# A perceiver block on one core: the first two rounds of its pipeline re-ordered

## The reference

```
# 1  cross attention to a context of 128 rows, 16 heads of 32, low rank
x = x + softmax(((LN(x) @ Wq_d) @ W_qk per head) @ (ctx @ Wkv_d).T / sqrt(32)) @ ((ctx @ Wkv_d) @ Wv_u per head)
# 2  self attention, one head of 128
q, k, v = split(LN(x) @ Wqkv + bqkv)
x = x + softmax(q @ k.T / sqrt(128)) @ v @ Wo + bo
# 3  Hadamard transform, 4-bit activations, ternary weights
xh = LN(x) @ hadamard;  s = max|xh| / 7;   xq = clip(round(xh / s), -8, 7) * s
ws = mean|w| per row;   wq = ws * (+1 where w/ws > 0.5, -1 where w/ws < -0.5, else 0)
x = x + xq @ wq.T
```

## Time and profile before

| | |
|---|---|
| median of 3 runs | 330.17 us |
| the profiled execution | 330.35 us, span 328.6 us |
| TensorE busy | 313.8 us, 95% |
| weight loads | 224.2 us, 68% |
| VectorE busy | 239.7 us, 73% |
| ScalarE busy | 212.5 us, 65% |
| GpSimd busy | 88.5 us, 27% |
| granted TensorE clock | 0.998 |

### The profile page before, as it was taken

How to read it: one execution, slowest core, us unless ns; L and a number is a source line. 1 busy time by engine, 2 the same in 40 slices (tenths; PEclk the granted TensorE clock), 3 DMA queues, 4 the chain that set the end, 5 groups by cost and what they waited for, 6 DMA issues and landing times.

```text
span 328.6 us, 8501 instructions
## 1 busy us (share of the span) xinstructions
PE 313.8 (95%) x3157; PEld 224.2 (68%) x3172; DVE 239.7 (73%) x517; ACT 212.5 (65%) x581; POOL 88.5 (27%) x129
## 2 busy tenths in 40 slices
PE   8989799999999999999999999999999999899995
PEld 6765767767576867667675868677675768575754
DVE  1499548686977868786878778686868788786435
ACT  1485858586686768585776867685867858672210
POOL 2000634241232314242213323242422233232320
PEclk9999999999999999999999999999999999999999
DMA  7994003040402203030403012030302020000000
GB/s 229 281 384 140 27 2 128 3 160 0 162 5 75 86 34 128 31 129 0 160 0 129 31 62 98 32 128 29 131 2 68 0 67 2 32 3 32 0 34 32
DMA packets 13481, 25.25 MB, mean 77 GB/s; under 512 B 3216, under 2 KB 3984, under 8 KB 13456
## 3 DMA queue, kind: packets, MB, share of 16 engines
q1 hardware_dynamic: 13456, 24.91, 22.3%
HBM read 20.71 MB, written 4.19 MB: 76 GB/s over the span
## 4 chain that ended last, share of the span: by engine, by line
PE 63%; DVE 21%; issue 5%; ACT 4%; DMA 3%; SPq 2%; POOL 1%; DVEq 1%; POOLq 0%
PE ps L662 13%; PE ps L702 7%; PE ps L609 5%; PE ps L786 5%; DVE mx L426 4%; PE ps L771 4%; PE ps L679 3%; PE ps L706 3%; PE ps L796 3%; PE ps L751 3%; DMA w_rows<-weight 3%; DVE sum_a L435 3%; PE ps L617 2%; PE ps L634 2%; PE ps L641 2%
## 5 line engine op out<-in xcount | busy, mean ns | idle before, releaser
L305 ACT ACTIVATE prob<-ps,nmx,qk_scale 128x128 f32<-128x128 f32 x256 | 96.2, 466 | 52.7 <-DVE nmx L430 52.7
L662 PE MATMUL ps<-had_s,x3t 128*128 128x512 f32 x128 | 58.4, 599 | 0.9 <-ACT x3t L299 0.9
L426 DVE TENSOR_REDUCE mx<-ps 128x8 f32<-128x1024 f32 x32 | 39.0, 1218 | 13.4 <-PE ps L786 13.4
L662 PEld LDWEIGHTS ps<-had_s,x3t 128*128 128x128 f32 x128 | 23.0, 189 | 24.8 <-issue 23.0
L435 DVE TENSOR_REDUCE sum_a<-prob 128x8 f32<-128x1024 f32 x32 | 37.5, 1209 | 2.3 <-ACT prob L305 2.3
L299 ACT ACTIVATE prob_t<-ps 128x512 f32<-128x512 f32 x64 | 35.2, 622 | 5.4 <-PE ps L609 5.4
L609 PE MATMUL ps<-ident,prob 128*128 128x128 f32 x256 | 33.4, 273 | 0.9 <-ACT prob L305 0.8
L702 PE MATMUL ps<-x2t,wqkv_s 128*128 128x128 f32 x256 | 32.7, 281 | 0.8 <-ACT x2t L299 0.8
L292 POOL TENSOR_TENSOR res<-prod,x 128x512 f32<-128x512 f32 x15 | 19.0, 1268 | 50.5 <-DVE prod L539 50.5
L702 PEld LDWEIGHTS ps<-x2t,wqkv_s 128*128 128x128 f32 x256 | 29.8, 191 | 2.5 <-ACT x2t L299 1.5
L288 POOL TENSOR_TENSOR qk_scale<-aux,power 128x1 f32<-128x1 f32 x16 | 8.8, 551 | 81.4 <-DVE aux L505 81.4
(11 more groups left out here) (115 smaller groups left out, 564.7 us busy)
## 6 DMA issues: line engine op xcount, KB each, us to landing
ct<-ctx_cols SPq DMA_DIRECT2D x16, 512.0 KB, 3.7
xt<-x_cols SPq DMA_DIRECT2D x16, 256.0 KB, 2.6
xr<-x_rows SPq DMA_DIRECT2D x16, 256.0 KB, 3.8
y<-res SPq DMA_DIRECT2D x15, 256.0 KB, 2.0
w_rows<-weight SPq DMA_DIRECT2D x1, 1024.0 KB, 8.8
had_s<-hadamard SPq DMA_DIRECT2D x1, 1024.0 KB, 8.6
wqkv_s<-wqkv SPq DMA_DIRECT2D x1, 768.0 KB, 10.2
wqk<-w_qk SPq DMA_DIRECT2D x2, 128.0 KB, 4.0
```

The lines of the kernel that those rows point to most:

```text
L305: last = nc.scalar.activation(prob[:, h, :], ps[:, h // 4, (h % 4) * P:(h % 4) * P + P], ACT.Exp, bias=nmx[:, h:h + 1], scale=qk_scale[:])
L426: V.tensor_reduce(mx[:, h], ps[:, 2 * half:2 * half + 2, :].rearrange("p r (c k) -> p (r c) k", c=EC), AX.X, ALU.max).then_inc(done["mx"], 1)
L662: mm = pe.matmul(ps[:, B4, :], x3t[:, c, :], had_s[:, c, :], start=(c == 0), stop=(c == EC - 1))
```

## The change

Round 0: on TensorE the projection of pair 1 moves ahead of the transposes of pair 0, between 4 and 8 units of filler (10 before), and the scores of pair 1 ahead of u. ScalarE evicts `lat` first, and no longer q_t, ckv and the first quarter of prob_t, which DVE takes. DVE does the weight's sums and scales there, in pieces between its other work, and both halves of pair 1's maxima. The compares of `ternary()` move into round 1, behind the variance of x2; `second_max()` stands right behind them. The ternary transposes and their evictions move from the end of round 0 to the end of round 1, behind the scores of pair 2, and use bank B2 in place of B3. Some waits change with the banks.

```diff
@@ ScalarE
+                if isinstance(i, int) and i == 0:
+                    latents()
                 if cross:
                     after(act, done["nmx"], i * 2)
                     exps(0, 4)
...
-                    pt_copy(0)
+                    if not (isinstance(i, int) and i == 0):
+                        pt_copy(0)
                     pt_copy(1)
...
-                if isinstance(i, int) and i == 0:
-                    for half, bank in ((0, B4), (1, B3)):
+                if self_:
+                    after(act, made["o2t"], i - 1)
+                    after(act, made["wo"], i - 2)
+                    copy(o2t[:], ps[:, B3, 0:P]).then_inc(read["o2t"], 1)
+
+                if isinstance(i, int) and i == 1:
+                    for half, bank in ((0, B4), (1, B2)):
                         act.wait_ge(ternt_made, half + 1)
@@ DVE (weight_sizes, weight_scales: the parts of ternary() by those names, the second with const_row;
@@      row_variance, row_scale, second_max: lines 497 to 510 as functions)
-                if cross:
+                if cross and not (first and i == 1):
                     largest(i, 1)
-                if isinstance(i, int) and i == 0:
+                if first and i == 0:
                     dve.wait_ge(ld_w["b"], 64)
                     V.tensor_copy(bv_wide[:], b_qkv[:, 2:3].to_broadcast([P, P])).then_inc(bvw_done, 1)
+                    dve.wait_ge(made["qt"], 2)
+                    V.tensor_copy(q_t[:], ps[:, B2, :].rearrange("p (c b q) -> p b c q", c=EC, b=2)).then_inc(read["qt"], 1)
+                    dve.wait_ge(made["ckv"], 2)
+                    V.tensor_copy(ckv[:, 1], ps[:, B1, 0:2 * SKV]).then_inc(read["ckv"], 1)
+                    sums(0)
+                    dve.wait_ge(made["pt"], 1)
+                    V.tensor_copy(prob_t[:, 0, :, :], ps[:, 0, :].rearrange("p (c t) -> p c t", c=EC)).then_inc(read["pt"], 1)
+                    row_variance()
+                    weight_sizes()
+                    dve.wait_ge(done["exp"], 2)
+                    row_scale()
+                    sums(1)
+                    dve.wait_ge(made["s"], 2)
+                    largest(1, 0)
+                    largest(1, 1)
+                    weight_scales()
+                if first and i == 1:
                     ternary()
-                    dve.wait_ge(cb_made, 1)
-                    V.tensor_tensor(const_row[:], ps[:, B4, :], bo_row[:], ALU.add).then_inc(const_ready, 1)
+                    second_max()
@@ TensorE
             def hadamard_mean():
                 pe.wait_ge(ld_w["had"], 16)
-                pe.wait_ge(ternt_read, 1)
+                pe.wait_ge(const_ready, 1)
...
             def ternary_transposed(half, bank):
                 pe.wait_ge(tern_done, EC)
                 if half == 0:
-                    pe.wait_ge(const_ready, 1)
+                    pe.wait_ge(row_read, 1)
                 else:
-                    pe.wait_ge(read["ckvk"], 1)
+                    pe.wait_ge(read["u"], 2)
...
                 if front:
+                    if first and i == 2:
+                        pe.wait_ge(ternt_read, 2)
                     pe.wait_ge(ld_xt[1 - par], (k + par + 1) * 16)
...
                 if cross:
                     if first and i == 0:
-                        keep_busy(10, B1)
+                        keep_busy(4, B4)
+                        after(pe, read["lat"], i + 1)
+                        projected()
+                        keep_busy(8, B4)
                     transposed(0)
                     transposed(1)
                 if first and i == 0:
-                    after(pe, read["lat"], i + 1)
-                    projected()
                     wide_bias()
...
+                if first and i == 0:
+                    scores()
+                if cross:
+                    weighted_sum()
...
-                if first and i == 0:
+                if front and not (first and i == 0):
+                    scores()
+                if first and i == 1:
                     ternary_transposed(0, B4)
-                    ternary_transposed(1, B3)
+                    ternary_transposed(1, B2)
```

More of the change, by code:

```diff
@@ L311, in pt_copy, with latents @@
                     copy(prob_t[:, r, :, :], ps[:, r, :].rearrange("p (c t) -> p c t", c=EC)).then_inc(read["pt"], 1)
+                def latents():
+                    after(act, made["lat"], i + 1)
+                    copy(lat[:], ps[:, B2, 0:P + 2 * SKV]).then_inc(read["lat"], 1)
+                if isinstance(i, int) and i == 0:
+                    latents()
                 if cross:
@@ L321, in body @@
                     exps(4, 8).then_inc(done["exp"], 1)
-                if front:
-                    after(act, made["lat"], i + 1)
-                    copy(lat[:], ps[:, B2, 0:P + 2 * SKV]).then_inc(read["lat"], 1)
+                if front and not (isinstance(i, int) and i == 0):
+                    latents()
                 if cross:
@@ L377, in body @@
                     copy(u_t[:], ps[:, B2, :].rearrange("p (c t) -> p c t", c=EC)).then_inc(read["u"], 1)
-                if isinstance(i, int) and i == 0:
-                    for half, bank in ((0, B4), (1, B3)):
-                        act.wait_ge(ternt_made, half + 1)
-                        copy(tern_t[:, 2 * half:2 * half + 2, :],
-                             ps[:, bank, :].bitcast(BF16).rearrange("p (c o) -> p c o", c=2)).then_inc(ternt_read, 1)
                 if self_:
@@ L386, in body @@
                     copy(o2t[:], ps[:, B3, 0:P]).then_inc(read["o2t"], 1)
+                if isinstance(i, int) and i == 1:
+                    for half, bank in ((0, B4), (1, B2)):
+                        act.wait_ge(ternt_made, half + 1)
+                        copy(tern_t[:, 2 * half:2 * half + 2, :],
+                             ps[:, bank, :].bitcast(BF16).rearrange("p (c o) -> p c o", c=2)).then_inc(ternt_read, 1)
             looped(act, body)
@@ L401, in _, with weight_sizes, weight_scales @@
             V.tensor_copy(fold4[:], fold[:].unsqueeze(1).to_broadcast([P, 4, LAT])).then_inc(fold_made, 1)
-            def ternary():
+            def weight_sizes():
                 dve.wait_ge(ld_w["w"], 16)
                 V.tensor_reduce(w_abs[:], w_rows[:], AX.X, ALU.add, apply_absolute_value=True).then_inc(wabs_done, 1)
+            def weight_scales():
                 dve.wait_ge(wabs_done, 1)
@@ L411, in ternary @@
                 V.tensor_copy(w_wide[:], w_scale[:].unsqueeze(2).to_broadcast([P, EC, P])).then_inc(wide_done, 1)
+                dve.wait_ge(cb_made, 1)
+                V.tensor_tensor(const_row[:], ps[:, B4, :], bo_row[:], ALU.add).then_inc(const_ready, 1)
+            def ternary():
                 dve.wait_ge(whalf_done, 1)
@@ L421, in body @@
             def body(i, k, par, front, cross, self_, quant):
+                first = isinstance(i, int)
                 def largest(pair, half):
@@ L435, in sums, with row_variance, row_scale, second_max @@
                     V.tensor_reduce(sum_a[:, h], prob[:, h, :], AX.X, ALU.add).then_inc(done["sum"], 1)
+                def row_variance():
+                    dve.wait_ge(ld_xr[1 - par], (k + par + 1) * 16)
+                    after(dve, made["lat"], i + 1)
+                    V.bn_stats(stat1[:], xr[:, 1 - par]).then_inc(done["stat1"], 1)
+                    dve.wait_ge(ld_w["wq"], 16)
+                    after(dve, done["stat1"], i + 1)
+                    V.bn_aggr(mv1[:], stat1[:]).then_inc(done["mv1"], 1)
+                def row_scale():
+                    after(dve, done["mv1"], i + 1)
+                    after(dve, done["qk_scale"], i)
+                    V.tensor_scalar(aux1[:], mv1[:, 1:2], EPS, float(LAT), ALU.add, ALU.mult).then_inc(done["aux1"], 1)
+                def second_max():
+                    after(dve, made["s2"], i - 1)
+                    V.tensor_reduce(mx2[:], ps[:, B3, 0:SQ], AX.X, ALU.max).then_inc(done["mx2"], 1)
+                    after(dve, done["mx2"], i - 1)
+                    V.tensor_scalar(nmx2[:], mx2[:], -float(D2) ** -0.5, None, ALU.mult).then_inc(done["nmx2"], 1)
                 if self_:
@@ L487, in body @@
                     V.tensor_scalar(qi[:], z[:], ROUND, QMAX, ALU.subtract, ALU.min).then_inc(done["qi"], 1)
-                if cross:
+                if cross and not (first and i == 0):
                     after(dve, done["rsum"], i - 1)
@@ L495, in body @@
                         .then_inc(read["qit"], 1)
[L496 to L510, removed]
+                if front and not (first and i == 0):
+                    row_variance()
+                    row_scale()
+                if self_ and not (first and i == 1):
+                    second_max()
                 if cross:
@@ L631, in body @@
                     if first and i == 2:
-                        pe.wait_ge(row_read, 1)
+                        pe.wait_ge(ternt_read, 1)
                     for c in range(EC):
```

(20 more changed lines are left out.)

## The result

The changed kernel takes 329.23 us, median of 8 runs, against 330.14 for the kernel before (8 runs): a ratio of 0.996, 95% interval 0.9945 to 0.9975. It is 0.9 us faster. Two later comparisons of the same two kernels gave more: 328.9 against 330.64 (0.9939, 0.9917 to 0.9961) and 328.66 against 330.15 (0.9954, 0.9938 to 0.997).

What follows compares the result with a forecast made beforehand. Round 1 was taken as bound by DVE's order, with TensorE full from round 2. 2.4 us sooner less 0.9 for transposes gives 1.5: 330.35 - 1.5 = 328.85, or 328.7 against the median 330.17; range 328.0 to 330.5.

Steps and rivals of the forecast that it cites:

- DVE's run up to xm: Round 0, DVE from the first transposed quarter: 9.45 us of work, so xm starts at 27.95, 1.95 sooner.
- GpSimd's delay by the compares: Round 1: the moved compares on DVE hold GpSimd off before x2n; taken as 0.2 us.
- Rival A: Round 1: rstd and x2n each wait behind a whole compare; gain only 0.5 to 0.8, 329.5 us; chance 0.15.
- Rival B: Round 1: DVE's compares hold the port throughout, x2n ends about 36.6; 2.7 us slower, 332.9; chance 0.08.
- x2t no longer behind the third exponentials: Round 1, ScalarE: exponentials over by about 30, x2t follows x2n at once; L702 at 33.9, 2.4 us sooner.
- Ternary transposes, 0.9: End of round 1, TensorE: 16 moved transposes add 0.9 us where it has no slack.
- The rounds behind carry the shift: From round 2 on TensorE is full, so the shift reaches the end unchanged; rounds again 18.0 us apart.
- The cover of the scores: Round 0: pair 1's scores are ready 0.5 us before DVE's first maximum asks, so they cost nothing.
- the cover of second_max: Round 1: compares end at 35.9, second_max is asked for at 38.9; 3.0 us spare, 1.2 more before TensorE sees it.
- rival C: Round 1: GpSimd's work pushes the compares, second_max late; at the outside 1.4 us slower, 331.6, priced 330.2; chance 0.09.
- stretch: From the first maximum on DVE to the start of round 2 on TensorE; predicted change -1.5 us.

Runs made afterwards that it cites:

- compares back: Changed kernel with the four compare pairs again in round 0, ahead of xm: 6.4 us over the changed kernel's median.
- sums first: Changed kernel with DVE's first sums of round 1 ahead of the compares, not behind second_max: slower than the kernel before, second_max 3.2 us late.
- maximum back: Changed kernel with the second half of pair 1's maxima again behind aux2 in round 1: 32.75 us from first maximum to round 2, against 32.81.
- v2: Changed kernel with maximum back, ScalarE evicting prob_t's first quarter again, and scales and const_row before pair 1's scores: median 327.24 us.
- second profile: Kernel before, run once more unchanged: start 1.1 us sooner, round 2 0.83 later, 281.62 us from round 2 to the end.
- third profile: Changed kernel, run again unchanged: first maximum at 11.61, 33.28 us from there to round 2.

## Why the prediction was right

**DVE's run up to xm**, 9.45 us from the first transposed quarter, and with it xm 1.95 sooner: measured 1.99. The quarter was copied from 20.01 to xm at 29.41, 9.4 us. The copy took 0.69, so const_row's 0.68 was the right row to take.

**GpSimd's delay by the compares**, taken as 0.2: rstd 0.72 instead of 0.55 and x2n 0.82 instead of 0.77, 0.22 together. The Trainium skill, page "SBUF — State Buffer", section "Who interferes with whom", says that when an instruction of DVE needs the ports that it shares with GpSimd, whichever of the two engines issues first has them for its whole instruction, and the other waits. The trace agrees in that both engines are held: GpSimd by the 0.17 and 0.05 above, and DVE, whose second L431 took 1.65 for 0.75 beside x2b. Rival A priced a whole compare for each of the two, and that did not come: rstd was issued 0.16 into a compare of 0.48 and x2n 0.57 into one of 0.75, and both lost less than what was left of it. Rival B did not come either.

**x2t no longer behind the third exponentials**: L742 1.36 behind L708 instead of 2.05, and 2.44 sooner in all. **Ternary transposes, 0.9**: measured 0.89 by doubling them.

**The rounds behind carry the shift**: round 2 takes 17.98 (17.99 before). TensorE is not full in all of them, as I had it from the windows in round 2: the first round of each turn of the loop takes 18.3 to 18.7 in both kernels. That changed nothing, since both kernels have it.

**The cover of the scores**, put at 0.5, was 0.14: they end at 24.72, and the first maximum of pair 1 starts at 24.86. It was still enough.

**Mis-sized, with no harm: the cover of second_max.** I gave it 3.0 us, from compares of 5.2. They took 8.45 (32.01 to 40.46), and 5.2 again in compares back, with no GpSimd instruction beside them: I had charged the port to GpSimd's side and only bounded DVE's in rival C. The question came at 40.29, the answer began at 40.38. The cover was nothing, and what was left was ScalarE's 1.1. Three experiments went over it (sums first, maximum back, v2), one into a loss. C, with a chance of 0.09, was the rival whose mechanism came nearest to coming true: GpSimd pushed the compares by 3.25, where C had 7.1 at the outside.

**Not in the forecast:** the rest of the program, 0.5 shorter; and what the two kernels hang on. The kernel before waits for the later of the weight's DMA (0.58 in the earlier trace rows, 2.54 in its second profile) and the first maxima. With that wait out of the way its stretch is 33.73, so 0.67 of the 1.59 was freedom from the DMA and 0.92 order. The changed kernel follows the first maximum, which started anywhere from 11.6 to 14.0 in three profiles of it, and where that is early it waits for the rows of pair 1 instead (0.37 in the third). I took 12.55 and the landings for fixed. That the one profile I counted from had a wait of 0.58 and not of 2.54 was luck: against the stretch of 36.36 in the second, the same change is worth 3.5. The median of the first comparison came 0.6 short of the forecast gain of 1.5, that of the second 0.2 over, and that of the third on it. All three stay below the 2.1 that the two profiles show from the first maximum on, of which 0.5 was not in the forecast. So the forecast total came out partly by luck: the 0.5 is in it unforeseen, and something took 0.35 to 1.2 back. The first median, 329.23, lies even nearer to rival A's 329.5 than to 328.7, but A's mechanism is not in the rows above. Later starts, or waits for the rows, are large enough for that, but most executions behind the medians have no profile, and it stays open.

## What to carry to other kernels

Find the first instruction that both profiles share and count from it, before comparing any later time; one profile of each is not enough where a start varies by more than the gain. Work taken off a path changes what the path hangs on: ask which landing or start is next, and how much it scatters. If compares on DVE move beside GpSimd's elementwise work, charge the delay to both engines: here DVE lost 3.25 (8.45 for 5.2), and GpSimd 1.0 (0.22 in rstd and x2n, 0.16 in x2b, 0.63 in the four centring steps).

## What was not expected of the hardware

The start scatters mostly because TensorE rises to full speed at different times. L721 of round -1, the same two instructions, first in the profile of the changed kernel, then in its third:
```profile
10.56 1.06 PE L721 MATMUL ps<-lat,fold 128*128 128x256 f32 x2
```
```profile
9.16 0.60 PE L721 MATMUL ps<-lat,fold 128*128 128x256 f32 x2
```
The scores behind them took 1.60 in the first and 1.20 in the third. The granted clock reads 1.00 in all windows there, as in this one of the changed kernel (last columns: granted clock, DMA share, GB/s), so that column does not show the start; durations do.
```profile
10.00:11.00 1.00, 1.00 (x6) 0.91 (x6) 0.00 (x0) 0.19 (x1) 0.39 (x1) 1.00 0.70 201
```
Later it does: in the second profile of before it fell to 0.50 behind 2.07 us of idle time, with L598 at 1.87 instead of 1.05, while 2.02 us of idle time ahead of L669 in the first had no such effect (L702 behind it took 2.05).
